# Tail exponentials stacked in rows, and the next group's head scores ahead of the values, in a gated cross-attention block

## What is computed

```python
x = x + tanh(g_xattn[0]) * xattn(layernorm(x), ctx)
x = x + tanh(g_ffn[0]) * ffn(layernorm(x))

# xattn: 16 heads of 32
scores = einsum('bqhd,bkhd->bhqk', Q, K) / sqrt(32)
out = einsum('bhqk,bkhd->bqhd', softmax(scores), V).reshape(B, T_q, D) @ Wo.T

# ffn, with x_prev the tokens moved on by one
r = sigmoid((mu_r * x + (1 - mu_r) * x_prev) @ W_r.T)
k = relu((mu_k * x + (1 - mu_k) * x_prev) @ W_k.T) ** 2
out = r * (k @ W_v.T)
```

## Time and profile before

| | before |
|---|---|
| median of 3 runs | 1349.93 us |
| lowest, highest | 1349.72, 1353.97 us |
| the profiled execution, whole | 1352.5 us |
| its span | 1350.8 us |
| PE, PEld busy | 98%, 73% |
| DVE, ACT, POOL busy | 77%, 58%, 49% |
| granted PE clock | 0.997 |

### The profile page before, as it was taken

One profiled execution on the slowest core, in us unless ns is written; L12 is line 12 of the kernel. 1 busy time (PEld: TensorE's weight loads), 2 busy tenths in 40 slices (PEclk: granted clock), 3 DMA queues, 4 the chain that ended last, 5 costly groups with the idle time before them and its releaser, 6 DMA issues.

```text
span 1350.8 us, 28900 instructions
## 1 busy us (share of the span) xinstructions
PE 1324.2 (98%) x9776; PEld 992.8 (73%) x9776; DVE 1046.6 (77%) x1983; ACT 778.0 (58%) x1457; POOL 659.6 (49%) x843
## 2 busy tenths in 40 slices
PE   6999999999999999999999999999999999999998
PEld 5667687777768677776877768777776877768777
DVE  6878778787886878778787887878788687877763
ACT  7655737466474655737466473745737465573633
POOL 7524445454444545445454445545445554444434
PEclk9998999999999999999999999999999999999999
DMA  9521312424123242312424222242413324231011
GB/s 311 155 59 48 91 51 78 116 55 128 44 84 77 62 132 54 99 45 77 112 54 132 59 77 66 62 132 54 122 33 85 93 54 139 54 92 48 32 48 40
DMA packets 160732, 113.27 MB, mean 84 GB/s; under 512 B 107456, under 2 KB 122304, under 8 KB 160704
## 3 DMA queue, kind: packets, MB, share of 16 engines
q1 hardware_dynamic: 160704, 112.91, 29.3%
HBM read 72.43 MB, written 35.39 MB: 80 GB/s over the span
## 4 chain that ended last, share of the span: by engine, by line
PE 88%; DVE 8%; ACT 3%; issue 1%; DMA 0%; DVEq 0%; ACTq 0%
PE g_bank L1415 41%; PE g_bank L1606 10%; PE o_bank L1546 7%; PE g_bank L1502 6%; PE s_bank L1520 4%; PE d_bank L1552 4%; PE s_bank L1530 3%; PE s_bank L1415 3%; PE s_bank L1478 3%; DVE buf L1006 2%; DVE o_bank L1194 2%; PE o_bank L1421 1%; DVE d_bank L1194 1%; PE s_bank L1524 1%; PE d_bank L1421 1%
## 5 line engine op out<-in xcount | busy, mean ns | idle before, releaser
L1099 DVE TENSOR_TENSOR pq<-s_bank,pq 128x512 f16<-128x512 f32 x320 | 220.0, 688 | 73.4 <-ACT s_bank L798 72.1
L1095 DVE TENSOR_REDUCE mm<-s_bank 128x3 f32<-128x462 f32 (+1 forms) x384 | 198.8, 578 | 74.6 <-PE s_bank L1478 74.6
L797 ACT ACTIVATE pq<-s_bank 128x512 f16<-128x512 f32 x320 | 194.3, 607 | 101.2 <-PE s_bank L1524 101.2
L798 ACT ACTIVATE s_bank<-s_bank 128x512 f32<-128x512 f32 x320 | 197.0, 616 | 0.0
L1606 PE MATMUL g_bank<-buf,WkT 128*128 128x512 f32 x720 | 189.7, 409 | 3.4 <-DVE buf L1006 3.3
L1415 PE MATMUL g_bank<-WrT,buf 128*128 128x512 f32 x744 | 183.7, 396 | 0.0
L1415 PE MATMUL g_bank<-WoT,buf 128*128 128x512 f32 (+1 forms) x768 | 175.4, 374 | 0.0
L1415 PE MATMUL g_bank<-WvT,buf 128*128 128x512 f32 x708 | 174.3, 395 | 0.0
L1415 PEld LDWEIGHTS g_bank<-WrT,buf 128*128 128x128 f32 x744 | 137.2, 188 | 39.3 <-issue 10.8
L1606 PEld LDWEIGHTS g_bank<-buf,WkT 128*128 128x128 f32 x720 | 131.4, 191 | 43.9 <-DVE buf L1006 9.6
L1415 PEld LDWEIGHTS g_bank<-WvT,buf 128*128 128x128 f32 x708 | 130.7, 188 | 32.4 <-issue 5.4
(11 more groups left out here) (186 smaller groups left out, 2304.6 us busy)
## 6 DMA issues: line engine op xcount, KB each, us to landing
xa<-in_x SPq DMA_DIRECT2D x64, 256.0 KB, 4.2
x<-in_x SPq DMA_DIRECT2D x64, 256.0 KB, 2.8
xt_scratch<-xa SPq DMA_DIRECT2D x28, 512.0 KB, 3.1
xnT_loaded<-xt_scratch SPq DMA_DIRECT2D x112, 128.0 KB, 3.2
out<-x SPq DMA_DIRECT2D x48, 256.0 KB, 2.3
place<-x SPq DMA_DIRECT2D x16, 256.0 KB, 2.4
out<-place SPq DMA_DIRECT2D x16, 256.0 KB, 2.0
k_all<-k_scratch SPq DMA_DIRECT2D x15, 256.0 KB, 3.3
```

The source lines that it names most:

```text
L797: nc.scalar.activation(pq[:, n, HI, :], bank[:, :], ACT.Exp, scale=SCALE).then_inc(p_hi, 1)
L798: nc.scalar.activation(bank[:, :], bank[:, :], ACT.Exp, scale=SCALE).then_inc(p_full, 1)
L1095: nc.vector.reduce_max(maxima, scores, AX.X).then_inc(reduced, 1)
L1099: nc.vector.tensor_tensor(pq[:, n, LO, :], score_bank[5 * g + n][:, :], pq[:, n, HI, :], ALU.subtract).then_inc(p_lo, 1)
```

## The change

The tails' rounded and lower exponentials had a tile of 128 rows each. Now both stand in each of two tiles: of heads 0 and 1 (rows 0 to 63 of the bank) the rounded part in rows 0 to 63 and the lower part in rows 64 to 127 of the first tile; of heads 2 and 3 the other way round in the second. One matmul over 128 rows then takes rounded and lower part together. `v_tail`'s HI part is loaded in both row places (eight DMAs for four), and `ones_tail` has ones in both. For it `exps` writes two instructions of 64 rows by 512 and waits for them ahead of the full one, and `p_low` does two of 64 rows.

`values` falls from 40 to 32 matmuls. In loop blocks the exponentials of even groups go to a second buffer `p_even` (over the storage of `xnT`), `head_scores(g+1)` stands ahead of `values(g)`, `tail_scores` of groups 1 to 3 stands within the first feed-forward product (after its third matmul), `attend(g-1)` stands behind the first `p_low` of group g, and `attn_high(g-1)` behind the group's last exponential. `mm` is packed into 140 columns.

```diff
             def exps(i, g, n, ffn):
...
-                later(act, av_done, i * G + g)
-                nc.scalar.activation(pq[:, n, HI, :], bank[:, :], ACT.Exp, scale=SCALE).then_inc(p_hi, 1)
+                later(act, av_done, i * G + g - 1 if ffn else i * G + g)
+                place = p_place(ffn, g, n)
+                if n < 4:
+                    nc.scalar.activation(place[:, HI, :], bank[:, :], ACT.Exp, scale=SCALE).then_inc(p_hi, 1)
+                else:
+                    for tile, rows in enumerate(tail_halves):
+                        nc.scalar.activation(place[rows, tile, :], bank[rows, :], ACT.Exp, scale=SCALE).then_inc(p_tail_hi, 1)
+                    act.wait_ge(p_tail_hi, 2 * (i * G + g + 1))
                 nc.scalar.activation(bank[:, :], bank[:, :], ACT.Exp, scale=SCALE).then_inc(p_full, 1)
...
-                nc.vector.tensor_tensor(pq[:, n, LO, :], score_bank[5 * g + n][:, :], pq[:, n, HI, :], ALU.subtract).then_inc(p_lo, 1)
+                    for tile, rows in enumerate(tail_halves):
+                        ins = nc.vector.tensor_tensor(place[tail_halves[1 - tile], tile, :], bank[rows, :], place[rows, tile, :], ALU.subtract)
+                    ins.then_inc(p_lo, 1)
...
+                for s in (HI, LO):
+                    for j in range(4):
+                        nc.tensor.matmul(o_bank[rows(j), :], v_tail[:, s, g, j, :], places[4][:, j // 2, :], start=False, stop=s == LO)
...
+                for j in range(4):
+                    ins = nc.tensor.matmul(d_bank[rows(j), :], ones_tail[:, j, :], places[4][:, j // 2, :], start=False, stop=True)
...
                 for j in range(4):
                     rows = slice(DH * j, DH * j + DH)
+                    other = slice(DH * ((j + 2) % 4), DH * ((j + 2) % 4) + DH)
...
+                    sp.dma_start(v_tail[other, HI, :, j, :], tails[:, HI, :, j, :]).then_inc(v_loaded, 16)
...
+                head_scores(i, 1)
                 values(i, 0, not ffn)
...
+                    ffn_r(i - 1, 1, at(1, lambda: tail_scores(i, 1)))
+                    ffn_v(i - 1, 0)
```

More of the change, by code:

```diff
@@ L72, in flamingo_block @@
             parts(n) for n in ("WqT", "WoT", "WrT", "WkT2", "WvT2"))
+        with nc.sbuf_tensor("p_even", [P, 4, 2, N], F16) as p_even:
+            pass
         xnT_loaded, xnT = parts("xnT")
@@ L114, in flamingo_block, with p_place @@
         recip = sb("recip", [P, N // 32], F32)
+        def p_place(ffn, g, n):
+            if ffn and g % 2 == 0:
+                return p_even[:, n, :, :] if n < 4 else p_even_tail[:, :, :]
+            return pq[:, n, :, :]
+        tail_halves = (slice(0, 2 * DH), slice(2 * DH, P))
         k2 = (place[:, 0, :], place[:, 1, :])
@@ L372, in load_values @@
                     rows = slice(DH * j, DH * j + DH)
-                    sp.dma_start(v_tail[rows, :, :, j, :], vt_scratch[b].rearrange("r s (g j d) -> r s g j d", g=G, j=4)[:, :, :, j, :]).then_inc(v_loaded, 16)
+                    other = slice(DH * ((j + 2) % 4), DH * ((j + 2) % 4) + DH)
+                    tails = vt_scratch[b].rearrange("r s (g j d) -> r s g j d", g=G, j=4)
+                    sp.dma_start(v_tail[rows, :, :, j, :], tails[:, :, :, j, :]).then_inc(v_loaded, 16)
+                    sp.dma_start(v_tail[other, HI, :, j, :], tails[:, HI, :, j, :]).then_inc(v_loaded, 16)
                 sp.dma_start(v_main[:, :, :], v_scratch[b]).then_inc(v_loaded, 16)
@@ L494, in _ @@
                                          base=DH - 1, pattern=[[DH, 4], [0, DH]], channel_multiplier=-1))
+            for first, last, base in ((0, 2, -2 * DH), (2, 4, 0)):
+                further = ones_further[:, first:last, :]
+                link(nc.gpsimd.memset(further, 1.0))
+                link(nc.gpsimd.affine_select(out=further, in_=further, compare_op=ALU.is_ge, fill=0.0,
+                                             base=base - OVER, pattern=[[-DH, 2], [0, DH]], channel_multiplier=1))
+                link(nc.gpsimd.affine_select(out=further, in_=further, compare_op=ALU.is_ge, fill=0.0,
+                                             base=DH - 1 - base, pattern=[[DH, 2], [0, DH]], channel_multiplier=-1))
+            link(nc.gpsimd.tensor_tensor(ones_tail[:, :, :], ones_tail[:, :, :], ones_further, ALU.add))
             link(nc.gpsimd.memset(tail_rows[:, :], 1.0))
@@ L873, in step @@
                     xr_high(i - 1, 2)
-                exps(i, 0, 0)
-                exps(i, 0, 1)
+                exps(i, 0, 0, ffn)
+                exps(i, 0, 1, ffn)
                 if ffn:
@@ L890, in step @@
                 for g in range(1, G):
-                    exps(i, g, 0)
-                    exps(i, g, 1)
-                    attn_high(i, g - 1)
+                    exps(i, g, 0, ffn)
+                    exps(i, g, 1, ffn)
+                    if not ffn:
+                        attn_high(i, g - 1)
                     if not ffn and g == 3:
@@ L897, in step @@
                         xT_high(i + 1, 0)
-                    exps(i, g, 2)
-                    exps(i, g, 3)
+                    exps(i, g, 2, ffn)
+                    exps(i, g, 3, ffn)
                     if not ffn and g < 3:
                         kv_high(FIRST_LATER + 2 * g)
-                    exps(i, g, 4)
+                    exps(i, g, 4, ffn)
+                    if ffn:
+                        attn_high(i, g - 1)
                     if ffn and pre:
@@ L1263, in step @@
                 for g in range(1, G):
-                    attend(i, g - 1)
-                    p_low(i, g, 0)
-                    p_low(i, g, 1)
+                    if not ffn:
+                        attend(i, g - 1)
+                    p_low(i, g, 0, ffn)
+                    if ffn:
+                        attend(i, g - 1)
+                    p_low(i, g, 1, ffn)
                     if ffn and pre and g == 2:
@@ L1509, in maxima_transposed @@
                 later(pe, x2_ready, i * TT - 1)
-                transposed(mT_bank, [mm[:, t, :] for t in range(TT)]).then_inc(mT_done, 1)
+                transposed(mT_bank, [mm[:, 4 * t:4 * t + P] for t in range(TT)]).then_inc(mT_done, 1)
             def head_scores(i, g):
@@ L1541, in values @@
                     pe.wait_ge(xT_lo, TT + 1)
[L1542 to L1553 removed]
+                places = [p_place(not by_pe, g, n) for n in range(5)]
+                for k, (s, q) in enumerate(PRODUCTS):
+                    for j in range(4):
+                        nc.tensor.matmul(o_bank[rows(j), :], v_main[:, s, DH * (4 * g + j):DH * (4 * g + j + 1)], places[j][:, q, :],
+                                         start=k == 0, stop=False)
+                for s in (HI, LO):
+                    for j in range(4):
+                        nc.tensor.matmul(o_bank[rows(j), :], v_tail[:, s, g, j, :], places[4][:, j // 2, :], start=False, stop=s == LO)
+                for q in (HI, LO):
+                    for j in range(4):
+                        nc.tensor.matmul(d_bank[rows(j), :], ones_main[:, :], places[j][:, q, :], start=q == HI, stop=False)
+                for j in range(4):
+                    ins = nc.tensor.matmul(d_bank[rows(j), :], ones_tail[:, j, :], places[4][:, j // 2, :], start=False, stop=True)
                 ins.then_inc(av_done, 1)
```

101 lines of the change are left out of this document (44 added, 57 removed).

## The result

| | before | changed |
|---|---|---|
| median | 1351.95 us (4 runs) | 1375.74 us (4 runs) |
| lowest, highest of the changed kernel | | 1373.1, 1377.18 us |
| ratio, 95% interval | | 1.0172, 1.0153 to 1.0191 |
| span of the profiled execution | 1350.8 us | 1375.5 us |

What follows compares the result with a forecast made beforehand. PE, busy 98% of the span, was taken as the bound. Fourteen loop blocks at +0.70 us (+9.8), block 15 (-0.2) and block 0 (+4.8) gave +14.4 us, so 1364.3 us on the 1349.93 median, range 1341 to 1380.

Steps and rivals of the forecast that it cites:

- The wait at group 1's head scores: Loop block: PE waits for the divided tail on ACT and DVE ahead of head_scores(1), 1.09 us (0.9 to 1.2).
- The tail scores: Loop block: PE waits for the first p_low ahead of group 1's tail scores, 0.43 us (0 to 0.6).
- Group 3's head scores: Loop block: group 2's later DVE work, turns included, makes PE wait ahead of them, 0.58 us (0.2 to 0.8).
- The way through DRAM: End of attention: turns 1.12 us later delay the next block's input, so PE's maxima wait 0.36 us on average (0 to 0.8).
- The saving: Values in a loop block: eight matmuls fewer a group, 0.44 us each group, 1.76 us a block.
- The 0.1 us a group: Scores directly beside values on PE: the changed tiling order could cost about 0.1 us either way per group.
- Block 0: First block, where PE waits for DVE at each group's values: longer chains less savings, +4.8 us (3 to 6).
- the tail's chain is 1.27 longer: Block 0: the tail's work ahead of PE's scores lengthens by 1.27 us, counted in three rounds and once ahead of the first.
- Before the first mark: Setup up to PE's first transpose of the maxima: no change forecast, 0 us.
- Half price for half rows: Rival: 64 rows cost half of 128 on ACT and DVE, the waits vanish, 1325 us; chance 0.16.
- only the first wait stays: Rival: tail scores, group 2's head scores and maxima find their operands, 1345 us, about no change; chance 0.12.
- DVE as the bound in groups 2 and 3: Rival: the divided tail costs DVE 0.4 us more in each of three groups, kernel at 1381 us; chance 0.10.

Runs made afterwards that it cites:

- the new order alone: The changed kernel with the tails as before (40 matmuls in values), only the new order of work and second exponential buffer kept: 1361.05 us, ratio 1.0062.
- the filled kernel: The changed kernel with three products of block 0 computed twice, 36 matmuls more than needed, ahead of PE's long waits: 1371.98 us, ratio 1.0136.
- the second profile of before: The kernel before, unchanged, profiled once more: span 1351.5 us, block 0 81.53 us.
- the stacked tails alone: The changed kernel with the order of work of before and one exponential buffer, tails still stacked: 1414.23 us, ratio 1.0448.
- the fastest one: Kernel before with stacked tails, main matmuls ahead of the tail's wait, attend and attn_high later, side work spread, next block's columns split otherwise: 1333.98 us, ratio 0.9861.

## Why the prediction was right in sign and place, and too small

**The wait at group 1's head scores** (1.09 forecast): start to start 637.70 - 633.65 = 4.05 us, where the same product takes 2.83 (616.18 to 619.01 in before): 1.22. The difference lies in the pairs of 64 rows. On DVE I stepped by 0.60 us; two take 1.39, and the next instruction starts 1.42 behind the first (52.64, 54.06), so 0.7 each. That is the rule of the Trainium skill which the prediction set against its sum (VectorE: DVE Perf Modes, Two Vector instructions with no wait between them); the trace agrees with it. On ACT the pair takes 1.20, and the full exponential starts 1.23 behind it, against 1.17 in my sum.

**The tail scores** (0.43): from head scores to head scores are 10.03 us (637.70 to 647.73), where 10.01 - 0.43 would be 9.58, so 0.45. Of these 0.19 are there with the old tails too. **Group 3's head scores** (0.58): 3.39 us for 2.82, 0.57. **The way through DRAM** (0.36): the seven blocks with no wait at the maxima take 81.05 us on average, all 14 take 81.42, so 0.37. **The saving** (1.76): 4 x 0.43. Together +0.89 for the measured +0.91, and +0.70 forecast. The 0.1 us a group that the prediction left open for scores and values side by side was not needed (3.41 us for 3.40 in the new order alone). What failed in the loop was a size: 0.13 at the first wait and 0.04 in the saving; the other terms are within 0.02. 14 times the difference of 0.21 is the 3 us.

**Block 0** (4.8 forecast, 10.3 measured) holds the step that failed. As waits it was right: three of 2.37 for 0.9, one of 1.69 for 0.28, two of 0.24 for none, less the saving, is +4.5. The step "the tail's chain is 1.27 longer" counted time in which PE stands and forgot what PE does afterwards: the stretches behind the four long waits take 6.2 us more at the lower clock than at full, as the filled kernel shows. Waits and clock are 10.7 us. Against the second profile of before, block 0 is 12.85 us longer: of the rest, 1.3 us are a lower clock at its end, which the kernel before has in its first profile too, and 0.8 remain. Most of that lies at the tail scores of groups 1 and 2: with a wait of 0.24 in the row, the way past them (58.58 to 62.86) is 0.5 us longer than before. Against the first profile of before, whose clock at that end was lower still (1.2 us), the difference is the 10.3. As the clock behind such waits was not the same in all executions, part of the 10 us is a matter of the execution.

**Before the first mark** (0): held. The 1.7 us also lie between two executions of the kernel before.

**The rivals.** Half price for half rows fell with the stacked tails alone. That only the first wait stays fell too, since the turns came 1.15 us late. DVE as the bound in groups 2 and 3 did not come in the changed kernel, but it came twice on the way to the fastest one, first as a ring with ACT and then with its turns in group 2.

**What the prediction did not ask** is whether the saving could be had in another way. It could, for 1.4 us of the 1.76 a block: with main matmuls ahead of the tail's wait, `attend` out of the exponentials' way, and DVE's and GpSimd's side work placed anew. Head scores ahead of the values stood against it: with the same side work, that order has 80.42 us a block for 79.1. The two kernels also differ in the main matmuls ahead of the tail's wait, and the runs do not separate these two.

## What to carry to other kernels

Splitting an instruction over rows cost a whole instruction on ACT and on DVE here; before it is done to save matmuls, lengthen the chain on paper and look for PE work that does not need its end, and put that work ahead of the wait rather than work that needs it. Where PE waits for nothing, as here, taking work from it shortens the kernel only as far as each ring over the other engines is shorter than PE's turn: write each as a sum per turn, and expect to meet several. A wait on PE has a second price where the clock falls behind it, so a wait of two microseconds may be better filled with work done twice (3.8 us gained here).

## What was not expected of the hardware

- Block 0 has seventeen PE waits of 2.31 to 2.54 us, in nine kernels. Over the 3.6 us behind them the granted clock was 0.53 to 0.69 sixteen times and 1.00 once (behind 2.54 us, the longest). Behind waits of 0.9 us it stayed at 1.00. Behind the last values' waits of 1.69 or 1.70 us it was 0.53 to 0.57 in three kernels and 1.00 in two. Behind waits of 1.25 to 1.38 us it was 1.00 in one execution of the kernel before and 0.50 or 0.66 in another. Which it is, the length of the wait alone does not tell.
- The same 48 matmuls, scores and values, take 4.49 to 4.56 us behind those waits in the changed kernel and 2.98 in a loop block (637.70 to 640.68).
- Two DVE instructions of 64 rows whose outputs start in different rows take 1.39 us, two of 128 rows in the same place 1.28. Two on ACT take 1.20 us with half the rows each, where full exponentials start 0.48 to 0.52 us apart.
